# Routing scores in groups, an earlier placement chain, and exponentials in another order: one change in two stages of a fused four-stage kernel

## The reference

```python
# block 2
scores = x @ router                                  # 8 scores a token
gates = sigmoid(top-1 score), 0 for the others
mid = silu((gates * x) @ w1[e]) * ((gates * x) @ w3[e])
out = silu(x @ ws1) * (x @ ws3) @ ws2 + sum_e mid @ w2[e]     # hidden width 352

# block 3
x, z = split(norm(seq) @ in_proj)
x = silu(conv4(x)); x_dbl = x @ x_proj               # 8 for dt, 16 for B, 16 for C
dt = softplus(x_dbl[:8] @ dt_proj + b)
h = h * exp(dt * A) + dt * x * B ;  y = h @ C + D * x         # scan over time
out = seq + res_scale * (y * silu(z)) @ out_proj
```

## Time and profile before

| | us |
|---|---|
| median of 3 runs | 2151.02 |
| lowest and highest | 2146.39, 2151.92 |
| the profiled execution, its own time | 2162.77 |
| its span | 2160.8 |
| TensorE busy | 1943.4 (90%) |
| VectorE busy | 1721.3 (80%) |
| ScalarE busy | 1633.7 (76%) |
| GpSimd busy | 1269.7 (59%) |
| mean granted TensorE clock | 0.953 |

### The profile page before, as it was taken

How to read it: one execution, slowest core, us unless ns; L and a number is a source line. 1 busy time by engine, 2 the same in 40 slices (tenths; PEclk the granted TensorE clock), 3 DMA queues, 4 the chain that set the end, 5 groups by cost and what they waited for, 6 DMA issues and landing times. The chain is left out here.

```text
span 2160.8 us, 40582 instructions
## 1 busy us (share of the span) xinstructions
PE 1943.4 (90%) x9574; PEld 1244.2 (58%) x9574; DVE 1721.3 (80%) x4049; ACT 1633.7 (76%) x5245; POOL 1269.7 (59%) x2141
## 2 busy tenths in 40 slices
PE   4999999999999999999999778669995899999996
PEld 2455555555555555555555546335663677777775
DVE  4799999899979998999999552567886677777774
ACT  3688888888878888888888523279991688888884
POOL 2367677667756766767676633518894545444550
PEclk9799999999989999999999879769997999999999
DMA  1000000000000000000000041112232000000000
GB/s 47 1 1 4 2 20 2 5 9 13 4 2 17 4 4 3 20 2 4 12 9 1 1 141 52 41 32 87 90 106 76 1 1 1 1 1 1 1 1 20
DMA packets 30366, 45.41 MB, mean 21 GB/s; under 512 B 9337, under 2 KB 21889, under 8 KB 29809
## 3 DMA queue, kind: packets, MB, share of 16 engines
q1 hardware_dynamic: 28864, 40.00, 5.9%
q0 software_dynamic: 1248, 2.59, 0.4%
HBM read 38.82 MB, written 5.32 MB: 20 GB/s over the span
## 5 line engine op out<-in xcount | busy, mean ns | idle before, releaser
L405 ACT ACTIVATE a_prob<-a_scores,a_negmax 128x256 f32<-128x256 f32 x1536 | 704.9, 477 | 132.0 <-DVE a_negmax L506 109.6
L506 DVE TENSOR_REDUCE a_negmax<-a_scores 128x2 f32<-128x512 f32 x768 | 521.7, 680 | 77.7 <-PE a_scores L628 62.4
L628 PE MATMUL a_scores<-a_km,a_qT 32*128 32x512 f32 x1536 | 444.2, 657 | 17.5 <-issue 8.9
L639 PE MATMUL a_heads<-a_prob,a_diag 128*128 128x256 f32 x1536 | 404.6, 397 | 43.2 <-DVE a_acc L514 41.3
L639 PEld LDWEIGHTS a_heads<-a_prob,a_diag 128*128 128x128 f32 x1536 | 278.6, 194 | 192.2 <-issue 96.8
L308 POOL TENSOR_TENSOR a_diag<-ident,a_rowinv 128x256 f32<-128x256 f32 x384 | 244.0, 635 | 181.9 <-DVE a_rowinv L547 174.4
L405 ACT ACTIVATION_READ_ACCUMULATOR a_prob<-a_scores,a_negmax 128x1 f32 x1536 | 322.1, 210 | 0.0
L628 PEld LDWEIGHTS a_scores<-a_km,a_qT 32*128 32x128 f32 x1536 | 117.5, 187 | 145.0 <-issue 110.6
L1424 DVE TENSOR_TENSOR_SCAN c_state<-c_decay,c_psD 128x1024 f32<-128x1024 f32 x64 | 146.1, 2286 | 35.6 <-PE c_psD L1541 35.0
L1257 POOL TENSOR_TENSOR c_du<-c_state,c_c_row 128x1024 f32<-128x1024 f32 x64 | 151.2, 2364 | 30.2 <-DVE c_state L1424 20.8
L1882 ACT ACTIVATE d_prob<-d_psS,d_bias,d_inv 128x128 f32<-128x128 f32 (+1 forms) x256 | 122.2, 487 | 27.6 <-DVE d_bias L2016 27.1
(11 more groups left out here) (291 smaller groups left out, 4172.1 us busy)
## 6 DMA issues: line engine op xcount, KB each, us to landing
c_c_row<-c_rows SPq DMA_DIRECT2D x32, 512.0 KB, 3.6
a_w<-in_a_w SPq DMA_DIRECT2D x12, 256.0 KB, 2.6
b_w<-in_b_w SPq DMA_DIRECT2D x1, 2816.0 KB, 14.2
a_rows<-in_a_rows SPq DMA_DIRECT2D x12, 128.0 KB, 2.0
b_w<-in_b_w SPq DMA_DIRECT2D x1, 1536.0 KB, 17.3
d_wqkv<-in_d_wqkv SPq DMA_DIRECT2D x2, 768.0 KB, 5.8
b_rows_in<-in_b_blank SPq DMA_DIRECT2D x1, 1518.0 KB, 8.8
b_packed<-b_rows_in SPq DMA_DIRECT2D x5, 264.0 KB, 4.2
```

The costliest lines, as they stand in the source:

```text
L405: ins = a.activation(prob[part % RING][:, c, :], psS[part % 2][:, c, :], ACT.Exp, bias=negmax[part % 2][:, c:c + 1], accum_out=rowsum[part ...
L506: v.tensor_reduce(negmax[part % 2][:, hs], psS[part % 2][:, hs, :], AX.X, ALU.max, negate=True).then_inc(s["negmax_ready"], 1)
L628: p.matmul(psS[part % 2][:, h * BH:(h + 1) * BH, :], qT[u][rows, t * P:(t + 1) * P], km[u][rows, c:c + BH, :], start=True, stop=True)\
L639: ins = p.matmul(psH[:, t, :], diag[part % RING][:, h, :], prob[part % RING][:, h * BH + 1, :], start=(j == 0 and h == 0), stop=(j == HG - ...
```

## The change

In the second stage the scores are made group by group (`route_scores(k)`), and turns 2 and 3 come between them, behind the wait for the constants. VectorE waits for all four increments. `product(2)` moves from ahead of the placement chain to behind `row_u`, ahead of the expert numbers.

In the third stage ScalarE's order of parts, low copies and exponentials is another, and TensorE's `turn_n(2)` and `turn_n(3)` move from behind `project_z(0, 1)` to ahead of `project_z(0, 0)`.

```diff
@@ stage_b, vector
-                v.wait_ge(s["scores_ready"], 1)
+                v.wait_ge(s["scores_ready"], NG)
...
                 product(0)
                 product(1)
-                product(2)
...
                 v.tensor_copy(row_u[:], row[:]).then_inc(s["routed"], 1)
-
+                product(2)
                 chain.link(v.tensor_tensor(passed[:], tile_no[:].unsqueeze(2).broadcast_to([P, MT, EXPERTS - 1]),
@@ stage_b, tensor
-                for k in range(NG):
+                def turn_x(k):
                     p.wait_ge(s["xn_ready"], k + 1)
                     if k >= 2:
                         p.wait_ge(s["xnT_ready"], k - 1)
                     for t in range(TPG):
                         ins = p.transpose(turn_bank[k % 2][:, t * P:(t + 1) * P], xn[:, k * TPG + t, :], ident[:])
                     ins.then_inc(s["turned"], 1)
+
+                def route_scores(k):
+                    p.wait_ge(s["xnT_ready"], k + 1)
+                    for t in range(k * TPG, (k + 1) * TPG):
+                        ins = p.matmul(psO[0][:, t * EXPERTS:(t + 1) * EXPERTS], xnT[:, t * P:(t + 1) * P], router[:],
+                                       start=True, stop=True)
+                    ins.then_inc(s["scores_ready"], 1)
+
+                turn_x(0)
+                turn_x(1)
                 p.wait_ge(s["const_in"], 144)
-                p.wait_ge(s["xnT_ready"], NG)
-                for t in range(T):
-                    ins = p.matmul(psO[0][:, t * EXPERTS:(t + 1) * EXPERTS], xnT[:, t * P:(t + 1) * P], router[:],
-                                   start=True, stop=True)
-                ins.then_inc(s["scores_ready"], 1)
+                for k in range(NG):
+                    route_scores(k)
+                    if k + 2 < NG:
+                        turn_x(k + 2)
@@ stage_c, scalar
                 for k in range(NG):
                     gate(k)
-                    if k >= 2:
-                        parts(k - 2)
+                    if k == 2:
+                        parts(0)
                     if k >= 1:
                         low_copy(k - 1)
-                low_copy(NG - 1)
-                parts(NG - 2)
-                for k in range(NG - 1):
+                parts(1)
+                exps(0)
+                low_copy(3)
+                exps(1)
+                for k in range(2, NG):
+                    parts(k)
                     exps(k)
-                parts(NG - 1)
-                exps(NG - 1)
@@ stage_c, tensor
                 for k in range(NG):
                     for t in range(DT):
                         project_x(k, t)
+                        if k == t == 0:
+                            for j in range(2, NG):
+                                turn_n(j)
                         project_z(k, t)
-                    if k == 0:
-                        for j in range(2, NG):
-                            turn_n(j)
```

## The result

| | before | changed |
|---|---|---|
| median, 11 runs each | 2146.57 us | 2138.72 us |
| lowest, highest | 2142.86, 2155.52 | 2130.14, 2148.53 |
| ratio, 95% interval | | 0.9956 (0.9937 to 0.9976) |
| profiled execution, its span | 2162.77, 2160.8 | 2134.78, 2132.9 |

The kernel became faster by 0.44%, with 0.24 to 0.63% as the interval; forecast was 0.37%, which lies in it. The time itself was forecast badly. The measured median, 2138.72, is 4.4 us under the 2143.1 named, at the very edge of the range (its lower end is 2138.5); 0.9956 of the 2146.57 us that the kernel before takes here is 2137.1 us, outside it. (The ratio is not the quotient of the two medians, which is 0.9963.) Of the experiments' runs on one chip, one of the kernel before took 5676.56 us and one of the kernel e7 3253.38; the ratios leave both out as slow.

What follows compares the result with a forecast made beforehand. Bounds: in the second stage scores, placement, 16 scatters and packed rows; in the third ScalarE's late exponentials. Gains of 1.4 + 2.1 = 3.5 and 4.4 us sum to 7.9; 2151.0 - 7.9 = 2143.1 us, range 2138.5 to 2149.5.

Steps and rivals of the forecast that it cites:

- 2151.0 - 7.9: Whole kernel: median of the runs then known, 2151.02 us, less the two stages' gain, giving 2143.1 us.
- Scores per group: Second stage, TensorE: scores interleaved with turns 2 and 3 end 1.4 us earlier, bounds 1.0 to 1.8.
- Placement ahead of product(2): Second stage, VectorE: the placement chain starts right behind product(1), 2.1 us earlier; its own 3.9 us stay.
- 0.9 us less: Second stage, TensorE's clock: if its step comes one product pair later, the gain is 0.9 us less.
- some 0.4 us later: Second stage: the wait moves from hidden(5) to hidden(4), so the shared expert ends some 0.4 us later, near 1303.9.
- The scatter waits for the row cast: Second stage, GpSimd: scatters wait for the row cast, 0.99 us from its end, not for the expert numbers.
- Exponentials: Third stage, ScalarE: the new order starts the exponentials, and VectorE's first block, 4.4 us earlier.
- rival (d): Third stage, ScalarE: each of six crossings adds a 1.28 us table load; total gain 1.2 us, 2149.8; chance 0.03.
- Moved turns: Third stage, TensorE: turns 2 and 3 ahead of the first z product give 0; bounds 0.5 lost, 1.16 won.
- Rival (c): Second-stage tiles: TensorE's clock also stays up, up to 2 us more; total gain 10 us, 2141; chance 0.08.
- rival (b): Only one stage delivers: second's gain eaten, 2146.6, or third's reduced, 2144.5 to 2147.5; chance 0.22.
- Rival (e): Third-stage scans: starting earlier against the clock's steps, five further low-clock steps make it 7 us slower, 2158; chance 0.05.

Runs made afterwards that it cites:

- e7: The changed kernel with TensorE's turns 2 and 3 of the third stage back in their old place, second chip; ratio to the kernel before 1.0004.
- e1: The kernel before, unedited, run again against itself on the first chip; ratio 1.0003.
- e2: The changed kernel, unedited, run again on the first chip; ratio to the kernel before 0.9964.
- e9: The kernel before, unedited, one run on the third chip for its trace; second stage 129.93 us, third 266.31 us.
- e10: The changed kernel, unedited, on the third chip; ratio to the kernel before 0.9957.
- e5: The kernel before with only product(2) moved behind the row numbers, second chip; ratio 1.0018.
- e11: The changed kernel with TensorE's third-stage turns 2 and 3 back in their old place, third chip; ratio to the kernel before 0.9975.
- e6: The kernel before with only TensorE's third-stage turns 2 and 3 moved ahead of the first z product, second chip; ratio 1.0006.
- e12: The changed kernel plus prefix products ahead of hidden(1) and placement right behind product(0), third chip; ratio to the kernel before 0.9950.
- e8: The changed kernel plus prefix products ahead of hidden(1) and placement right behind product(0), second chip; ratio to the kernel before 0.9977.

## Why the prediction was right and wrong

**The sum came out, and closer than the traces repeat.** 3.5 + 4.4 = 7.9 us were forecast, and the first two profiles show 3.53 + 4.35 = 7.88. That agreement is luck in part: e1 and e2 give 3.54 + 3.38 = 6.92, e9 and e10 4.11 + 5.53 = 9.64, and what moves them is TensorE's clock. The changed kernel's ratios, 0.9956, 0.9964 and 0.9957, have intervals that all hold the forecast 0.9963.

**The time was wrong, and the step that failed is the base in "2151.0 - 7.9".** It took the median of three runs as what the kernel takes. Sets of 11, 35, 35 and 22 runs of the same kernel have medians of 2146.57, 2146.52, 2146.55 and 2146.71. Three runs were 4.5 us too high, and the range gave the base less than 3 us. With the base of 11 runs the same sum gives 2146.57 - 7.9 = 2138.7, and 2138.72 was measured. That the 11.8 us between profile and median don't scale with these stages held: the first stage took 1248.2, 1232.2 and 1228.1 us in three traces of the kernel before, while its other stages moved by under 1 us each. What the forecast didn't draw from those 11.8 us is how far runs spread, 12 us and more in each set.

**Term by term.**

- Scores per group: 1.4 forecast, 1.6 measured at the score copy (18.79 to 17.19), in all traces with it; alone it left 1.0 at the stage's end.
- Placement ahead of product(2): 2.1 forecast from copy to row cast. e5 has 2.2; the changed kernel 1.7 (11.24 instead of 12.97) in its first trace and 2.9 in e2 (10.04), as TensorE's clock rose later or earlier under `hidden(1)`. The forecast had this as the clock's "0.9 us less"; in the first trace it was 0.4.
- The shared expert "some 0.4 us later": mis-sized. It was 2.0 later in the first trace and e10, since the stall at `hidden(4)` was followed by a stretch at the low clock, and 0.9 earlier in e2, where it wasn't and the clock had also risen earlier. It cost nothing, as packed_turn(1) still waited for transfers, but of a slack of 7.2 us only 1.6 to 1.7 was left in the first trace, e10 and e11, and 4.0 in e2; the forecast's own numbers leave 3.3.
- The scatter waits for the row cast: right, the releaser is now named so.
- Exponentials: 4.4 forecast. The order itself gave 4.38: from `gate(3)`'s last activation to the first block it is 5.89 to 5.90 us in all eight traces with the new order, and 10.2 to 10.3 in those with the old one but e5 (9.53). The whole stage gained 3.4 to 5.5 by pairs, as the clock ahead of it and in the scans varied. Margins held and no load was added: rival (d) is out. The Trainium skill's rule to batch by set ("ScalarE: Activation LUTs", Table sets: the hidden batching unit) did not bite, since the same section puts the cheap functions into every set. The trace agrees with that: the copy at 1399.68 and the Abs at 1401.20 ran between exponentials without a load.
- Moved turns: 0 forecast, 0.0 (e10 against e11) and 0.2 (e6) measured.
- Rival (c) came in e10, e11 and e12, with 1.25 us in e10. On the second chip it went further than rival (b): in e7 the second stage was not only robbed of its gain but 3.2 us longer than before, by a way that was on no list, a standstill of ScalarE. In e6, whose second stage is the old one, the delay was 6 us and fitted into the slack; in e5, e7 and e8 it was 8 to 13 us, more than even the old 7.2. Whether the old order keeps it short, or that one execution did, the traces don't show; that the kernel before is no slower on this chip speaks for the order. The forecast looked at slack only to see that it sufficed, not at what would use it up. Rival (e) didn't come: from the additions to the stage's end it is 204.8 us before and 205.0 after.

**Open.** What holds ScalarE on that chip. It ends some 3.7 us after the last scatter's start, and the scatters' landings are missing from the same traces, but no run tells whether the scatters cause it. The changed kernel itself was not run there; that it would give back its gain is inferred from e7, which has the same second stage and a ratio of 1.0004.

## What to carry to other kernels

Cut the profile into stages at fixed instructions and compare stage by stage: here three pairs gave 6.9, 7.9 and 9.6 us where whole executions of one kernel differ by 15. Take more than one pair before believing a tenth of a microsecond. Put the sum on a base only after asking how far the untouched parts vary, and give the range that width. And when a change draws the critical line forward, write down the slack that it takes from the work beside it: 7.2 us became 1.7, and on one chip in three the kernel of e7, with that slack, gained nothing.

## What the runs showed of the hardware

- The same first stage, with 5148 products, took 1227 to 1248 us. TensorE's busy time in it was 1105.6 to 1127.0, and it explains nearly all of that: 20.1 of 20.0 us between the first two traces.
- A wait of 1.95 us at `hidden(4)` was followed by a stretch at 1.2 GHz in the first trace (the next two products took 1.94 instead of 1.02 us) and by none in e2 (1.13). The same order of work may or may not pay for the clock. Likewise behind the wait of 1.2 us ahead of packed_turn(1): 0.60 granted in the first trace, 1.00 in e10.
- On one chip ScalarE stood still once for 11 to 13 us while GpSimd issued scatters, in three of four traces, and for shorter stretches in the fourth. The cause is open.
